# Turned z stored as two 16-bit parts, taken out through the ring banks; three z buffers and an early split of the output weights

## What is computed

```python
q, k, v = (einsum('bsd,dhk->bshk', resid, W) for W in (W_Q, W_K, W_V))
probs = softmax(where(causal, -1e6, einsum('bqhc,bshc->bhqs', q, k) / 8))
z = einsum('bhqs,bshc->bqhc', probs, v)
x = layernorm(resid + einsum('bqhc,chd->bqd', z, W_out) + b_out)
h = layernorm(x) * gamma + beta
y = silu(h @ dequant(fc1) + fc1_bias)
out = layernorm(x + x + 0.5 * (y @ dequant(fc2) + fc2_bias))
```

## Time and profile before

| | us |
|---|---|
| median of 3 runs | 2035.65 (2034.11 to 2035.74) |
| the profiled execution, its own time | 2037.36 |
| its span, first to last instruction | 2035.4 |
| attention, to its last `z_T` | about 1672 |
| feed-forward, from its first DMA | 1677 to 2035 |
| mean granted TensorE clock | 0.974 of full speed |

### The profile page before, as it was taken

How to read it: one execution, slowest core, us unless ns; L and a number is a source line. 1 busy time by engine, 2 the same in 40 slices (tenths; PEclk the granted TensorE clock), 3 DMA queues, 4 the chain that set the end, 5 groups by cost and what they waited for, 6 DMA issues and landing times. The chain is left out here.

```text
span 2035.4 us, 54700 instructions
## 1 busy us (share of the span) xinstructions
PE 1826.0 (90%) x22601; PEld 1299.9 (64%) x22601; DVE 1418.6 (70%) x2688; ACT 1520.9 (75%) x3151; POOL 1319.7 (65%) x738
## 2 busy tenths in 40 slices
PE   3788989999989898989899999999999977989997
PEld 2455756565656565656666666666666656878886
DVE  5886868676767676767767676768686838565663
ACT  3488887888888888888787878787879872654463
POOL 2365767686867686867676868686767786343242
PEclk8899999999999999999999999999999988999998
DMA  3002010101010101010101010101010205111210
GB/s 116 9 4 81 5 40 2 43 2 43 5 40 5 40 5 41 7 38 10 35 10 35 10 35 12 33 12 33 13 33 15 92 26 199 63 63 63 81 55 21
DMA packets 48647, 75.09 MB, mean 37 GB/s; under 512 B 5904, under 2 KB 32784, under 8 KB 48144
## 3 DMA queue, kind: packets, MB, share of 16 engines
q1 hardware_dynamic: 48400, 71.59, 11.2%
HBM read 33.82 MB, written 20.97 MB: 27 GB/s over the span
## 5 line engine op out<-in xcount | busy, mean ns | idle before, releaser
L459 POOL TENSOR_TENSOR p_lo<-p_full,p_hi 128x1024 f16<-128x1024 f32 (+1 forms) x640 | 1163.3, 1839 | 489.6 <-ACT p_full L507 489.2
L506 ACT ACTIVATE p_hi<-psum 128x512 f16<-128x512 f32 (+3 forms) x1280 | 721.7, 564 | 232.3 <-PE psum L774 123.0
L546 DVE TENSOR_REDUCE row_max<-psum 128x1 f32<-128x512 f32 (+3 forms) x1280 | 723.3, 604 | 98.3 <-PE psum L736 66.2
L507 ACT ACTIVATE p_full<-psum 128x512 f32<-128x512 f32 (+3 forms) x1280 | 729.1, 572 | 0.0
L794 PE MATMUL psum<-v,p_hi 128*128 128x65 f16 x4352 | 497.5, 193 | 36.3 <-DVE z_pair L591 34.1
L796 PE MATMUL psum<-v,p_hi 128*128 128x64 f16 x4352 | 499.9, 195 | 0.0
L798 PE MATMUL psum<-v,p_lo 128*128 128x65 f16 x4352 | 495.6, 192 | 0.0
L794 PEld LDWEIGHTS psum<-v,p_hi 128*128 128x128 f16 x4352 | 409.8, 96 | 102.5 <-issue 55.5
L768 PE MATMUL psum<-qa,ka 128*128 128x512 f16 (+3 forms) x1280 | 444.2, 348 | 24.6 <-ACT p_full L507 18.8
L772 PE MATMUL psum<-qb,kb 128*128 128x512 f16 (+3 forms) x1280 | 445.0, 348 | 0.0
L796 PEld LDWEIGHTS psum<-v,p_hi 128*128 128x128 f16 x4352 | 406.7, 97 | 55.4 <-issue 0.8
(11 more groups left out here) (126 smaller groups left out, 2991.9 us busy)
## 6 DMA issues: line engine op xcount, KB each, us to landing
zT_dram<-z_T SPq DMA_DIRECT2D x16, 1024.0 KB, 4.3
shared_z<-zT_dram SPq DMA_DIRECT2D x28, 512.0 KB, 6.3
qb<-qa SPq DMA_DIRECT2D x128, 64.0 KB, 1.9
ka<-ka SPq DMA_DIRECT2D x128, 64.0 KB, 1.9
shared_z<-xT_dram SPq DMA_DIRECT2D x8, 512.0 KB, 7.7
xs<-x_dram SPq DMA_DIRECT2D x8, 512.0 KB, 8.1
out_dram<-shared_w SPq DMA_DIRECT2D x8, 512.0 KB, 3.4
w_raw_rest<-wqkv_dram SPq DMA_DIRECT2D x1, 2304.0 KB, 14.6
```

The source lines that it names most:

```text
L459: nc.gpsimd.tensor_tensor(p_lo[:, at % NP, cols], p_full[:, at % NP, cols], p_hi[:, at % NP, cols], ALU.subtract).then_inc(probs_split, 1)
L506: nc.scalar.activation(p_hi[:, at % NP, to], lane_bank(a)[:, P * f:QB], ACT.Exp, scale=1.0 / SCORE)
L507: nc.scalar.activation(p_full[:, at % NP, to], lane_bank(a)[:, P * f:QB], ACT.Exp, scale=1.0 / SCORE).then_inc(lane_read, 1)
L546: nc.vector.reduce_max(row_max[:, n % MAXES, t, c:c + 1], bank_of(r)[:, 0:chunk_width(n, t, c)], AX.X).then_inc(ring_read, 1)
```

## The change

z leaves the attention as two 16-bit floats, without a scale. `out(m, q)` moves from the lanes to the ring: PE transposes into a ring bank, ACT copies it to the high half of `z_T` in 16 bits, DVE waits for that, subtracts it from the bank into the low half, and only that releases the ring bank. The DRAM tensor holds both parts, with as many bytes as before. The store of a unit is issued at step 6 of the next one.

The output weights are loaded in unit 3, multiplied there by a power of two per pair (V's), scaled by their peak and split into two 16-bit parts, on ACT and DVE, at steps 6 to 38. The powers of two that z no longer has are put in at one place, `z_power`, in the sum with `x` in `to_norms`.

The feed-forward part loads finished parts of z into three buffers, one DMA per block, and splits nothing of them: ACT's, POOL's and DVE's `split_z` and the split of the output weights at the start are gone. The output projection multiplies 16-bit parts.

```diff
-RING_AT = places(("chunk", "turn", "values", "group", "peaks", "scales"))
-LANE_AT = places(("scores", "out"))
+RING_AT = places(("chunk", "turn", "values", "group", "out", "peaks", "scales"))
+LANE_AT = places(("scores",))
...
+WO_UNIT, WO_PEAK_STEPS, WO_SPLIT_STEPS = 3, [6, 9, 12, 15], [26, 30, 34, 38]
+WO_PART = PAIRS // 4
+STORE_STEP = 6
...
+    if m == WO_UNIT:
+        steps[0].append(("load_wo", m))
+        for u, i in enumerate(WO_PEAK_STEPS):
+            steps[i].append(("wo_peak", m, u))
+        steps[20].append(("peaks", m, WO_PEAK, PEAKS))
+        steps[22].append(("scales", m, WO_PEAK, PEAKS))
+        for u, i in enumerate(WO_SPLIT_STEPS):
+            steps[i].append(("wo", m, u))
+    if m:
+        steps[STORE_STEP].append(("store", m - 1))
...
-        z_T = sb("z_T", [P, NQ, QB])
+        z_T = sb("z_T", [P, NQ, 2, QB], F16)
...   (ACT)
             def out_rows(m, q):
-                a = lane_place("out", m, q)
+                r = RING_AT[("out", m, q)]
                 reach(act, z_stored, 16 * m)
-                act.wait_ge(lane_ready, a + 1)
-                nc.scalar.activation(z_T[:, q, :], lane_bank(a), ACT.Copy,
-                                     scale=z_scale[:, m // PAIRS, m % PAIRS:m % PAIRS + 1]).then_inc(lane_read, 1)
+                act.wait_ge(ring_ready, r + 1)
+                nc.scalar.activation(z_T[:, q, 0, :], psum[:, RING + r % RINGS, :], ACT.Copy).then_inc(z_hi_done, 1)
+            def split_wo(u):
+                nc.scalar.activation(wo_parts[:, 0, g, :], wo_raw[:, g, :], ACT.Copy,
+                                     scale=scale[:, WO_PEAK:WO_PEAK + 1].bitcast(F32)).then_inc(wo_hi_done, 1)
...   (DVE)
+            def out_rows(r, m, q):
+                dve.wait_ge(z_hi_done, m * NQ + q + 1)
+                nc.vector.tensor_tensor(z_T[:, q, 1, :], bank_of(r), z_T[:, q, 0, :], ALU.subtract).then_inc(ring_read, 1)
+            def wo_peaks(m, u):
+                for g in range(g0, g0 + WO_PART):
+                    nc.vector.tensor_scalar(wo_raw[:, g, :], wo_raw[:, g, :], v_power[:, g, 2:3], None, ALU.mult).then_inc(wo_scaled, 1)
+                dve.wait_ge(wo_scaled, g0 + WO_PART)
+                nc.vector.tensor_reduce(wo_peak[:, u:u + 1], wo_raw[:, g0:g0 + WO_PART, :], axis=AX.XY, op=ALU.max,
+                                        apply_absolute_value=True).then_inc(peaked, 1)
+            def split_wo(u):
+                dve.wait_ge(wo_hi_done, u + 1)
+                nc.vector.scalar_tensor_tensor(out=wo_parts[:, 1, g, :], in0=wo_raw[:, g, :],
+                                               scalar=scale[:, WO_PEAK:PEAKS].bitcast(F32), in1=wo_parts[:, 0, g, :],
+                                               op0=ALU.mult, op1=ALU.subtract).then_inc(wo_split, 1)
...   (PE)
-            def turn_outputs(m, q):
-                a = lane_place("out", m, q)
+            def turn_outputs(r, m, q):
                 pe.wait_ge(z_done, m * NBLK + 2 * q + 2)
-                reach(pe, lane_read, a - LANES + 1)
+                bank = ring_bank(r)
...   (feed-forward, SP)
             def load_z(i):
-                for u in range(ZQ):
-                    sp.wait_ge(z_split, i * ZQ - ZQ + u + 1)
+                if i >= Z_BUFS:
+                    sp.wait_ge(wo_ready, i - Z_BUFS + 1)
                     sp.sem_inc(passed, 1)
-                    sp.dma_start(quarter(z_raw, u), zT_dram[bass.ds(i, 1), :, GQ * u:GQ * u + GQ, :] ...).then_inc(z_in[u], 16)
+                sp.dma_start(z_bufs[i % Z_BUFS] ..., zT_dram[i] ...).then_inc(z_in[i % Z_BUFS], 16)
...   (feed-forward, PE)
             def out_projection(i):
                 pe.wait_ge(wo_read, i + START)
+                if i:
+                    pe.wait_ge(z_in[i % Z_BUFS], 16 * (i // Z_BUFS + (i % Z_BUFS > 0)))
+                z = z_bufs[i % Z_BUFS]
                 for g in range(PAIRS):
-                    if g % GQ == 0:
-                        pe.wait_ge(z_split, i * ZQ + g // GQ + 1)
                     for t in range(TPB):
                         cols = slice(P * t, P * t + P)
-                        last = passes(psum[...], (z_hi[:, g, cols], z_lo[:, g, cols]), (wo_hi[:, g, :], wo_lo[:, g, :]), ...)
+                        last = passes(psum[...], (z[:, g, 0, cols], z[:, g, 1, cols]), (wo_parts[:, 0, g, :], wo_parts[:, 1, g, :]), ...)
...   (feed-forward, ACT)
-                    if more == 2 and f in Z_AT:
-                        split_z(i + 2, Z_AT[f])
...
-            act.wait_ge(early_in, 16 * 2)
-            for u in range(ZQ):
-                nc.scalar.activation(quarter(z_hi, u), quarter(z_raw, u), ACT.Copy).then_inc(z_hi_done, 1)
-            for u in range(ZQ):
-                split_z(1, u)
...   (feed-forward, POOL)
-            for i in range(2):
-                for u in range(ZQ):
-                    pool.wait_ge(z_hi_done, i * ZQ + u + 1)
-                    nc.gpsimd.tensor_tensor(quarter(z_lo, u), quarter(z_raw, u), quarter(z_hi, u).bitcast(F32),
-                                            ALU.subtract).then_inc(z_split, 1)
...   (feed-forward, DVE)
-                nc.vector.tensor_tensor(y[:, :, :], sums, xs[:, k, :, :], ALU.add).then_inc(wo_read, 1)
+                nc.vector.scalar_tensor_tensor(out=y[:, :, :], in0=sums, scalar=z_power[:, b:b + 1], in1=xs[:, k, :, :],
+                                               op0=ALU.mult, op1=ALU.add).then_inc(wo_read, 1)
...
-                    if more == 2:
-                        split_z(i + 2)
...
-            dve.wait_ge(early_in, 16 * 2)
-            split(Chain(wo_split, 0), wo_raw, wo_hi[:, :, :], wo_lo[:, :, :])
```

More of the change, by code:

```diff
@@ L240, in pair_order @@
     order += [("out", m, block_of(n)[1]) for n in range(1, NBLK, 2) if SLOTN[n] + LAG + 3 >= NSLOT]
-    return order + [("store", m)]
+    return order if more else order + [("store", m)]
 def first_order():
@@ L265, in places, with lane_place, attention @@
     return {x: r for r, x in enumerate(counted)}
-RING_AT = places(("chunk", "turn", "values", "group", "peaks", "scales"))
-LANE_AT = places(("scores", "out"))
+RING_AT = places(("chunk", "turn", "values", "group", "out", "peaks", "scales"))
+LANE_AT = places(("scores",))
 def peaks_before(at):
     seen = ORDER[:ORDER.index(at)]
[L275 to L282, removed]
+    whole = (("x_peak", NQ - 1), ("wo_peak", PAIRS // WO_PART - 1))
+    return sum((x[0] in ("w_peak", "x_peak", "wo_peak")) + ((x[0], x[-1]) in whole) for x in seen)
+def lane_place(m, i, u):
+    return LANE_AT[("scores", m, i, u)]
+def attention(nc, shared, z_power, early_in, wo_split, xT, wqkv, zT_dram, wout):
     with ExitStack() as ctx:
@@ L418, in _ @@
                     copy_group(m, *x)
+                if what == "load_wo":
+                    load_wo(m)
                 if what == "store":
@@ L528, in _ @@
                     out_rows(m, *x)
+                if what == "wo":
+                    split_wo(*x)
         @block.vector
@@ L632, in scales @@
                 w_powers = powers[:, 1:1 + 3 * PAIRS].rearrange("p (g k) -> p g k", k=3)
-                batch, pairs = (1, slice(0, PAIRS)) if c1 == PEAKS else (0, slice(max(0, c0 - 1) // 3, (c1 - 1) // 3))
+                if c0 == WO_PEAK:
+                    for b in range(B):
+                        last = nc.vector.tensor_scalar(z_power[:, b:b + 1], powers[:, X_PEAK[b]:X_PEAK[b] + 1], powers[:, c0:c1],
+                                                       0.125, ALU.mult, ALU.mult)
+                    step(last)
+                    dve.sem_inc(scaled, 1)
+                    dve.sem_inc(ring_read, 1)
+                    return
+                batch, pairs = (1, slice(0, PAIRS)) if c0 == X_PEAK[1] else (0, slice(max(0, c0 - 1) // 3, (c1 - 1) // 3))
                 if batch == 0:
@@ L637, in scales @@
                 x_power = powers[:, X_PEAK[batch]:X_PEAK[batch] + 1]
[L638 to L639 removed]
+                step(nc.vector.tensor_scalar(q_scale[:, batch, pairs], qk_power[:, pairs], x_power, x_power, ALU.mult, ALU.mult))
                 dve.sem_inc(scaled, 1)
@@ L674, in _ @@
                     outputs(m, *x)
+                if what == "out":
+                    out_rows(r, m, *x)
+                if what == "wo_peak":
+                    wo_peaks(m, *x)
+                if what == "wo":
+                    split_wo(*x)
                 if what == "x_peak":
@@ L1171, in to_norms @@
                                                op0=ALU.mult, op1=ALU.add).then_inc(first_norms, 1)
-            def split_z(i):
-                for u in range(ZQ):
-                    dve.wait_ge(z_hi_done, i * ZQ + u + 1)
-                    nc.vector.tensor_tensor(quarter(z_lo, u), quarter(z_raw, u), quarter(z_hi, u).bitcast(F32),
-                                            ALU.subtract).then_inc(z_split, 1)
             def to_hT(i):
```

117 lines of the change are left out of this document (64 added, 53 removed).

## The result

The changed kernel takes 2049.03 us (median of 14 runs, 2045.24 to 2052.17), the kernel before 2035.7 (14 runs, 2032.69 to 2044.98): a ratio of 1.0063, 95% interval 1.0053 to 1.0072. Forecast were 2026 us and a gain. The spans of the two profiled executions, 2047.8 and 2035.4, are compared in what follows.

What follows compares the result with a forecast made beforehand. PE, busy 90% of the span, was taken as the bound, with waits differing by part. Gained 50.7 less lost 41.3 gave 9.4 us net: 2028.0 from 2037.36, or 2026 against the median 2035.65; own range 2017 to 2037, wider range 2001 to 2048.

Steps and rivals of the forecast that it cites:

- Start of the feed-forward part: Before the first `fc1`: DVE's four operations after q1 lands fall from 14.44 to 6.20 us, 8.2 us gained.
- Steps 0 to 5: Feed-forward steps: without the z split each costs what step 6 does, 5.97 us less, 35.8 us gained for six.
- Rival C: Feed-forward steps gain only half, 3 us each, as table loads and norms replace the split: 2044 us; chance 0.09.
- 16-bit projection: Output projection in feed-forward: 0.96 us less for 96 matmuls, seven projections on the path, 6.7 us gained.
- The boundary: Between attention units: DVE waits for ACT's copy and subtracts, `turn` 1.8 us late, 27 us lost over 15 boundaries.
- Rival B: At the unit boundary: PE's later waits swallow the 1.8 us delay, 27 us come back: 1999 us; chance 0.19.
- Mid-unit outs: Outs inside attention units: delay under cover of two slots, 0.03 us each, 1.5 us lost for 48.
- Rival A: At every `out`: DVE's wait and subtraction cost 0.8 us at mid-unit outs too, slower, 2063 us; chance 0.17.
- Output weights in unit 3: Attention unit 3: multiplications, reductions, scale chain and splits add 22 us of DVE, 12 us lost, bounds 4 and 22.
- the factor of 0.59 us of PE for one of DVE: From unit 2: 11.2 us of DVE splits made it 6.6 us longer; used to price the work in unit 3.
- The 18.6 us in place of 10.4: Unit 3: if each multiplication waits out a POOL subtraction at the shared port, eight take up to 18.6 us, not 10.4.
- Lost 27 + 1.5 + 0.8 + 12 = 41.3: Attention losses in us: 27 boundaries, 1.5 mid-unit outs, 0.8 last unit's subtraction before the last store, 12 unit 3.

Runs made afterwards that it cites:

- Experiment 1: Changed kernel with the last `out` of a unit moved to step 4 of the next unit: 2027.05 us, ratio 0.996 to the kernel before.
- (4): Changed kernel with the k group of step 34 behind the outputs of block 6 on all engines: 2031.97 us, ratio 0.9983 to the kernel before.
- (7): Changed kernel with both halves of `z_T` written by DVE, no wait for ACT: 2043.04 us, ratio 1.0046 to the kernel before.
- (2): Kernel before with nine extra 512-column matmuls ahead of the group behind each unit's boundary: 2082.45 us, ratio 1.0229.
- experiment 11: Kernel before with the k group of step 34 behind the outputs of block 6 and nine extra matmuls a unit: 2074.52 us, one run.

## Why the prediction was wrong

Mechanism by mechanism it was right, and its sign was wrong, because one term was missing: TensorE's clock.

- *Start of the feed-forward part*: right. 8.2 forecast for DVE, 8.3 measured; the part up to the first `fc1` 8.6. The z load did come late for projection 1, by some 1.5 us, and the "7.06 us gap" fell to 4.51, which made up for it.
- *Steps 0 to 5*: right. 34.20 us a step, 34.3 forecast; no gap left at `a_lo`. Rival C is out.
- *16-bit projection*: right in the steps. 34.35 to 33.33 us in step 6, 1.02 for 96 matmuls (0.96 forecast). Projection 1 gained nothing: 13.26 us before at a granted clock of 0.87, 13.47 after at 0.78.
- *The boundary*: right. The turn is 1.74 us late (1.8 forecast). Rival B is out, nothing swallows it.
- *Mid-unit outs*: 101.08 - 99.16 - 1.74 = 0.2 us for three. Rival A is out at its price of 0.8 each. Experiment 1 takes 1.0 off with the place of the last `out` and leaves 0.9 for the rest, so the parting of the 1.9 is not firm; their sum is.
- *Output weights in unit 3*: right. DVE is busy for 94.41 - 74.24 = 20.2 us more and waits 2.4 for ACT in it, 22.6 where 22 were forecast. Unit 3 is 21.6 us longer than a unit without a drop; without 1.65 for each of its five drops (the double one counted twice) 13.3 remain, for 12 forecast. PE's added idle time, 12.4, says the same. Three other kernels with this work in unit 3 give 12.4 (experiment 1), 13.6 (4) and 13.5 (7) by the same subtraction. So the factor of 0.59 us of PE for one of DVE held. The duration of a multiplication was guessed in the middle of wide bounds and came out near, 1.37 us for 1.3; that is luck. The 18.6 us in place of 10.4, which the prediction held possible, did not come: it was 10.9.
- *The clock*: this is the step that failed. "Lost 27 + 1.5 + 0.8 + 12 = 41.3" has no term for it, which puts it at nothing, without a reason. The changed kernel has drops for 15 where the kernel before has 3: 12 x 1.65 = 19.8 us, 6.6 of them in the stalls of unit 3.

The ring lost 15 x 1.92 = 28.8, unit 3 13.3 and the clock 19.8: 61.9 of the 63.9 us. The two that the prediction had come to 42.1, for 27 + 1.5 + 12 = 40.5 forecast. The missing 20 are more than twice the forecast net gain of 9.4; without them the median would be some 2029 us (an estimate), close to the forecast of 2026. That a drop in a stall of unit 3 costs what it costs elsewhere is inferred; the four kernels agree with it within 1.2 us.

**In which units a drop comes.** Unit length and amount of work don't decide it, but the traces show more. Below is the time from the end of PE's 2 us pause to the start of the drop, unit by unit (a dash is a unit with the pause and without a drop):

| kernel | units | length with a drop | us from pause to drop |
|---|---|---|---|
| changed | 3 to 14 | 102.7 | 0.8, 0.5, 0.1, -, 1.2, 0.9, 0.5, 0.2, -, 1.2, 0.8, 0.5 |
| before, nine matmuls (2) | 4 to 13 | 102.8 | 1.2, 0.8, 0.4, 0.0, -, 0.9, 0.5, 0.1, -, 1.0 |
| experiment 11 | 4 to 13 | 102.1 | 0.1, 0.3, 0.7, 0.9, 1.2, -, 0.0, 0.3, 0.6, 0.9 |

In all three, drops of neighbouring units start 102.4 us apart. The pauses are 102.7 or 102.8 us apart in the first two, so the time between them shrinks unit by unit; in the third they are 102.1 apart, and it grows. At each dash the next start, 102.4 us on, would have fallen before the end of the pause (812.4 against 812.55 in the changed kernel) or, in experiment 11, 1.5 us behind it, and no drop came; the unit without one is 1.65 us shorter and sets the two against each other anew. So whether a pause of 2 us brings a drop goes by when it ends, to a fraction of a microsecond.

What stays open: what sets these instants, and why a kernel falls into a run of units with drops or stays out of one. Shown is that PE pauses ahead of each drop, that padding PE with work alone takes the count from 3 to 12, and that neither the length of a unit nor the place of the pause decides by itself. No kernel with the exact order of the changed one and without drops was made. Each drop count rests on one profiled execution.

## What to carry to other kernels

A result of 50 us gained and 60 lost looks like a change that did little: compare the traces part by part before judging it, and keep the part that gained. Before pricing a wait from the length of a stretch, look at the granted clock in it, and take PE's idle time apart from its busy time: a third of what unit 3 seemed to lose to DVE was the clock. Put added work in steps where its engine has room: the same work cost 13 us in one unit and 3 spread over nine. When an in-order engine waits for another engine's half of a job while holding a bank of a ring, move the entry to where the other engine is not late; that gained 22 us, doing both halves on one engine 6.

## What was not expected of the hardware

TensorE's granted clock fell from 2.4 to 1.2 GHz for a few microseconds behind pauses of about 2 us, at 1.65 us a time, in some units and not in others that did the same work in the same order. It fell 3 times in the kernel before, behind pauses of 2.01 to 2.10 us. In the changed kernel it fell 14 times, ten of them behind pauses of 1.94 us and four behind pauses of 2.7 to 4.2. With nine matmuls more in each unit of the kernel before it fell 12 times. Whether a 2 us pause brought a drop went by the instant at which it ended. A periodic kernel can so lose 0.7% (nine more drops, 15 of 2036 us, in that last kernel) by a change that gives PE no further pause.
